# A gated attention and feed-forward block: similarity rows loaded once in the opening, TensorE's opening reordered, and the up half's banks freed by ScalarE

## The reference, cut to what matters

```python
# x, ctx: 16 x 128 x 1024, float32
def xattn(feature, embedding, weight):            # weight: 128 x 128 x 3
    emb_l = shift_right(embedding)                # zeros come in at the edge
    emb_r = shift_left(embedding)
    sim = stack([cos(embedding, emb_l), cos(embedding, embedding), cos(embedding, emb_r)], axis=1)
    att = repeat(sim, C, axis=1)                  # one row per tap, the same for all 128 channels
    inp = stack([f_pad[:, :, k:k + T] for k in range(3)], axis=2).reshape(B, 3 * C, T)
    return einsum('bit,oi->bot', inp * att, weight.reshape(O, 3 * C))

def ffn(h, gate_w, up_w, down_w, fc1_w, fc2_w, expert_w, gamma, beta):
    routing_weights, _ = top_k(h @ gate_w, 2)
    shared = relu(h @ up_w) ** 2 @ down_w         # 1024 -> 2048 -> 1024
    latent = h @ fc1_w                            # 1024 -> 512
    routed = (latent @ expert_w) * routing_weights.sum(-1, keepdims=True) @ fc2_w
    return layernorm(shared + routed) * gamma + beta

x = x + tanh(g_xattn) * xattn(layernorm(x), ctx, weight)
x = x + tanh(g_ffn) * ffn(layernorm(x), ...)
```

## Time and profile before

| | |
|---|---|
| time, median of 3 runs | 1007.84 us (1005.25 to 1008.19) |
| the profiled execution | 1008.68 us, its span 1006.5 us |
| TensorE's mean granted clock | 0.985 |
| TensorE busy | 948.0 us, 94% of the span |
| VectorE, ScalarE, GpSimd busy | 484.1, 323.2, 324.5 us |
| TensorE in the first 100 us | busy 70.44 us |
| TensorE in the next two hundreds | busy 92.10 and 91.13 us |

### The profile page before, as it was taken

How to read it: one execution, slowest core, us unless ns; L and a number is a source line. 1 busy time by engine, 2 the same in 40 slices (tenths; PEclk the granted TensorE clock), 3 DMA queues, 4 the chain that set the end, 5 groups by cost and what they waited for, 6 DMA issues and landing times.

```text
span 1006.5 us, 12367 instructions
## 1 busy us (share of the span) xinstructions
PE 948.0 (94%) x4562; PEld 441.6 (44%) x4562; DVE 484.1 (48%) x845; ACT 323.2 (32%) x441; POOL 324.5 (32%) x149
## 2 busy tenths in 40 slices
PE   2898799969999999999999999999999999999995
PEld 1346544434444444444444444444444444444442
DVE  6366588896466244455574244455574222221112
ACT  2457777553322112233332112233332112211111
POOL 4250224045954233033763333033763200001110
PEclk9899999979999999999999999999999999999998
DMA  8797797323234354423225244422225222200001
GB/s 347 206 312 262 296 384 279 113 80 105 85 96 139 106 180 152 143 90 84 58 93 144 99 160 152 141 92 84 59 90 145 77 94 102 84 1 7 15 21 42
DMA packets 63999, 131.28 MB, mean 130 GB/s; under 512 B 35266, under 2 KB 35394, under 8 KB 62658
## 3 DMA queue, kind: packets, MB, share of 16 engines
q1 hardware_dynamic: 62786, 126.07, 38.7%
q10 hardware_dynamic: 1152, 4.39, 1.2%
HBM read 105.09 MB, written 19.07 MB: 123 GB/s over the span
## 4 chain that ended last, share of the span: by engine, by line
PE 81%; DVE 9%; ACT 2%; DMA 2%; issue 2%; DVEq 2%; POOL 1%; SPq 0%; ACTq 0%; POOLq 0%
PE psS L1328 31%; PE psR L1278 18%; PE psS L1278 16%; PE psR L1338 8%; PE psP L1246 5%; PE psP L1259 2%; DVE ring L1055 1%; DVE s L893 1%; DVE hid L1106 1%; DVE s L897 1%; DMA sim_scratch<-simo 1%; PE psR L1384 1%; DMA sim_side<-sim_scratch 1%; DVEq L1092 1%; ACT hid L765 1%
## 5 line engine op out<-in xcount | busy, mean ns | idle before, releaser
L1328 PE MATMUL psS<-big,hid 128*128 128x512 f16 x1536 | 337.6, 381 | 8.9 <-issue 8.6
L1328 PEld LDWEIGHTS psS<-big,hid 128*128 128x128 f16 x1536 | 150.5, 98 | 191.4 <-issue 11.7
L1278 PE MATMUL psS<-xT,ring 128*128 128x512 f16 (+1 forms) x912 | 191.7, 370 | 3.0 <-DVE xT L1001 1.7
L1278 PE MATMUL psR<-xT,ring 128*128 128x512 f16 (+1 forms) x912 | 190.0, 368 | 0.0
L1278 PEld LDWEIGHTS psS<-xT,ring 128*128 128x128 f16 x912 | 89.8, 99 | 102.5 <-issue 4.8
L1278 PEld LDWEIGHTS psR<-xT,ring 128*128 128x128 f16 x912 | 89.2, 98 | 97.2
L517 POOL TENSOR_TENSOR y<-y,lgb 128x1024 f32<-128x1024 f32 x15 | 39.3, 2617 | 251.7 <-ACT y L655 251.7
L1019 DVE SCALAR_TENSOR_TENSOR y<-psR,rw,y 128x1024 f32<-128x1024 f32 x15 | 19.2, 1282 | 140.6 <-PE psR L1338 140.6
L1338 PE MATMUL psR<-w,lgb 128*128 128x512 f16 x384 | 85.5, 379 | 0.0
L488 POOL TENSOR_TENSOR sides<-scr 128x1024 f32<-128x1024 f32 x12 | 29.3, 2440 | 141.6 <-DMA scr<-in_ctx 141.6
L507 POOL TENSOR_TENSOR ring<-f_buf,ring 128x1024 f32<-128x1024 f32 x18 | 39.2, 2177 | 100.8 <-ACT f_buf L623 68.8
(11 more groups left out here) (196 smaller groups left out, 989.0 us busy)
## 6 DMA issues: line engine op xcount, KB each, us to landing
ring<-pair_scratch SPq DMA_DIRECT2D x60, 512.0 KB, 3.4
ring<-sim_scratch SPq DMA_DIRECT2D x18, 504.0 KB
big<-in_w_up SPq DMA_DIRECT2D x8, 1024.0 KB, 13.7
out_rows<-y SPq DMA_DIRECT2D x15, 512.0 KB, 3.0
hid<-in_w_down SPq DMA_DIRECT2D x14, 512.0 KB, 7.7
big<-in_w_down SPq DMA_DIRECT2D x14, 512.0 KB, 8.2
pair_scratch<-ring SPq DMA_DIRECT2D x12, 512.0 KB, 7.0
sim_side<-sim_scratch SPq DMA_DIRECT2D x11, 504.0 KB
```

The costliest lines, as they stand in the source:

```text
L1278: mm = pe.matmul(up_bank[t % NR][:, cols], rows[:, a, k, :], xT[:, k, b, cols], start=(k == 0 and a == 0 and b == 0), stop=(k == KB - 1 an ...
L1328: mm = pe.matmul(psS[:, HALF * h:HALF * h + HALF], hT[:, i, a, P * j:P * j + P], dn[:, i, b, HALF * h:HALF * h + HALF], start=(i == 0 and ...
```

## The change

It has six parts.

1. The first block's similarity rows are read once: one broadcast of 504 KB for row j and the three edge pieces (`load_first_sims`). VectorE copies the broadcast to the other two taps' tiles (`copy_sims`, L958 after). The taps are taken in the order `T_FIRST`, GpSimd's second one and VectorE's behind a copy each.
2. The fc1 load goes from ScalarE's queue to SP's, behind the broadcasts of rows 0 to 2, and the loads of `w_up` come in another order.
3. TensorE's opening: the attention of row 0 stands ahead of the third fc2 product, the fourth one behind the first transposes, the transposes of row 2 ahead of the first latent half tiles, and the norm of `w_up` ahead of the first latent tile's second half.
4. ScalarE's and VectorE's openings are reordered to that: all four fc1 low halves stand ahead of `combine(0, 1)`.
5. In every up half ScalarE's Relu itself frees the bank. ScalarE then squares the Relu's result out of SBUF straight into the high half, VectorE squares the same buffer in float32 (L1111 after) and takes the low half (L1119 after). The shift constants follow.
6. In the first up half `w_down` rows 0 to 9 are split beside the tiles, rows 10 to 15 (before 13 to 15) behind `f_los`, and the split stands at the end of each tile's work. The first attention of block 1 stands behind ten steps of `shared` (before twelve), and each of these steps waits for its own hidden row and its own `w_down` row (before, the whole product waited for 14 hidden rows).

```diff
-HID_SHIFT = -45
+HID_SHIFT = -23
+    T_FIRST = (0, 2, 1)
-        DN_SPLIT = {13: (0, 2), 14: (2, 4), 15: (4, 6), 16: (6, 8), 17: (8, 10), 18: (10, 12), 19: (12, 13)}
-        DN_LATE = range(13, IT)
+        DN_SPLIT = {13: (0, 2), 14: (2, 4), 15: (4, 6), 16: (6, 8), 17: (8, 10)}
+        DN_LATE = range(10, IT)
-        XATTN_AT, XATTN_FIRST = (5, 0, 0, 0), (12, 12, 10, 6)
+        XATTN_AT, XATTN_FIRST = (5, 0, 0, 0), (10, 12, 10, 6)
...
+            def load_first_sims(j):
+                rows = sim_dram[:, T * j:T * j + T]
+                S = S_first[j % 3]
+                sp.dma_start(S[0][0:G * GROUP, :],
+                             rows.rearrange("(a g) t -> a g t", a=1).broadcast_to([GROUP, G, T]))\
+                    .then_inc(sim_first[j], 16)
+                for k, ends in enumerate((slice(0, 2), slice(0, 3, 2), slice(1, 3))):
+                    sp.dma_start(S[k][G * GROUP:, :], rows[ends, :]).then_inc(sim_first[j], 16)
...
             for j in range(3):
-                load_sims(0, j)
+                load_first_sims(j)
+            sp.dma_start(fc1_flat, w_fc1.rearrange("p t k -> p (t k)")).then_inc(f1_in, 16)
...
-                    for n, k in enumerate(T_ORDER[0:2]):
+                    for n, k in enumerate(T_FIRST[0:2]):
+                        if n == 1:
+                            pool.wait_ge(s_copied, 2 * j + 1)
...
-                        act.activation(buf, bank, ACT.Relu, scale=2.0 ** HID_SHIFT).then_inc(relu_rdy, 1)
+                        act.activation(buf, bank, ACT.Relu, scale=2.0 ** HID_SHIFT).then_inc(up_evac, 1)
-                    if first:
-                        for c in range(*DN_SPLIT.get(t, (0, 0))):
-                            dn_split_hi(c)
                     if t >= LT:
-                        act.wait_ge(sq_hid, i + 1)
-                        act.activation(hT[:, t - LT, 0, :], hbuf[:, t % 2, :], ACT.Copy).then_inc(h_hi, 1)
+                        act.drain()
+                        act.activation(hT[:, t - LT, 0, :], hbuf[:, t % 2, :], ACT.Square).then_inc(h_hi, 1)
...
-            act.dma_start(fc1_flat, w_fc1.rearrange("p t k -> p (t k)")).then_inc(f1_in, 16)
...
+            def copy_sims(j):
+                dve.wait_ge(s_sem(0, j), sims_loads(0, j))
+                for k in T_FIRST[1:]:
+                    dve.tensor_copy(s_of(0, j)[k][0:G * GROUP, :], s_of(0, j)[0][0:G * GROUP, :])\
+                        .then_inc(s_copied, 1)
...
                         i = IT * n + t - LT
-                        dve.wait_ge(relu_rdy, i + 1)
-                        dve.scalar_tensor_tensor(out=hbuf[:, t % 2, :], in0=bank, scalar=0.0,
-                                                 in1=hbuf[:, t % 2, :], op0=ALU.max, op1=ALU.mult)
-                        dve.drain().then_inc(up_evac, 1)
-                        dve.drain().then_inc(sq_hid, 1)
+                        dve.wait_ge(h_hi, i + 1)
+                        dve.tensor_tensor(hbuf[:, t % 2, :], hbuf[:, t % 2, :], hbuf[:, t % 2, :], ALU.mult)
...
             def first_up_half():
                 pe.wait_ge(xt_rdy, 2 * BB)
+                norm_over_rows(WUP, IT, 3)
                 for t in range(LT):
                     tile(slot(t), t, slice(PAIR, TOK)).then_inc(up_done, 1)
-                    if t == 0:
-                        norm_over_rows(WUP, IT, 3)
...
                     if first:
+                        pe.wait_ge(h_rdy, i + 1)
                         pe.wait_ge(dn_rdy, i + 1)
...
-                        pe.wait_ge(h_rdy, IT * (n + 1) - 2)
                         if first:
                             pe.wait_ge(w2_rdy, LT)
+                        else:
+                            pe.wait_ge(h_rdy, IT * (n + 1) - 2)
```

More of the change, by code:

```diff
@@ L465, in _ @@
             for k in range(2, 4):
+                load_up(k)
+            sp.wait_ge(w2_done, LT)
+            for k in range(6, 8):
                 load_up(k)
@@ L699, in up_half @@
                             act.drain().then_inc(dn_sq, 1)
+                        for c in range(*DN_SPLIT.get(t, (0, 0))):
+                            dn_split_hi(c)
                     if first and t in CTX_FIRST:
@@ L806, in _ @@
             act.drain().then_inc(amax_rdy, 1)
-            w2_evac(2)
-            f_rows(0, 2)
-            for l in range(3):
-                w2_squares(l)
             f_rows(0, 3)
@@ L813, in _ @@
             x1_normal(0, 0)
-            w2_evac(3)
+            w2_evac(2)
+            for l in range(3):
+                w2_squares(l)
             act.wait_ge(scale_rdy, 2)
@@ L825, in _ @@
                 up_square(it)
+            w2_evac(3)
+            w2_squares(3)
             first_xt_hi(1, 0)
@@ L829, in _ @@
             x1_normal(0, 2)
-            for it in range(12, IT):
+            for it in range(4, 8):
                 up_square(it)
+            first_xt_hi(2, 0)
+            first_xt_hi(2, 1)
             std(L1, 3)
             x1_normal(0, 3)
-            first_xt_hi(2, 0)
-            first_xt_hi(2, 1)
-            for it in range(4, 6):
+            for it in range(12, IT):
                 up_square(it)
@@ L839, in _ @@
             first_xt_hi(3, 1)
-            for it in range(6, 12):
+            for it in range(8, 12):
                 up_square(it)
@@ L1098, in up_half @@
                         tile_lo(EARLY + t)
-                    if first and t == SCALE_T:
-                        down_scale()
-                    if first:
-                        for c in range(*DN_SPLIT.get(t, (0, 0))):
-                            dn_lo(c)
                     if t >= LT:
-                        dve.wait_ge(h_hi, i + 1)
+                        dve.drain()
                         dve.tensor_tensor(hT[:, t - LT, 1, :], hbuf[:, t % 2, :], hT[:, t - LT, 0, :],
@@ L1109, in up_half @@
                         x_stats(m, 0)
+                    if first and t == SCALE_T:
+                        down_scale()
                     if phase_a and t == COS_T:
                         cosines(m)
+                    if first:
+                        for c in range(*DN_SPLIT.get(t, (0, 0))):
+                            dn_lo(c)
                     if first and t == SUM_T:
@@ L1192, in _ @@
             dve.drain().then_inc(scale_rdy, 1)
+            copy_sims(3)
+            fc1_los(0, LT)
+            combine(0, 1)
             weigh_last(3)
-            combine(0, 1)
             first_xt_lo(0, 0)
             first_xt_lo(0, 1)
-            fc1_los(0, 2)
             combine(0, 2)
@@ L1392, in _ @@
             norm_over_rows(WX, 2, 1)
+            xattn_first(0)
             expert_fc2(2)
-            xattn_first(0)
-            expert_fc2(3)
             norm_over_rows(WF1, 1, 2)
@@ L1399, in _ @@
             turn_first(0, 1)
+            expert_fc2(3)
             xattn_first(2)
```

55 lines of the change are left out of this document (29 added, 26 removed).

## The result

The changed kernel takes 1015.54 us (median of 4 runs, 1014.15 to 1016.12) against 1007.79 us before: 1.0088 times as long, with a 95% interval of 1.0064 to 1.0111. The forecast was 1014.5. The profiled execution after took 1014.15 us with a span of 1012.4, 5.9 us more than the span of before.

What follows compares the result with a forecast made beforehand. TensorE was taken as the bound, busy 948.0 of 1006.5 us. Opening +7.7, end of up half -0.4, loop -0.6 give +6.7: 1015.4 profiled, 1014.5 for the median, range 1001 to 1021.

Steps and rivals of the forecast that it cites:

- the opening: Start of the kernel up to the first hidden tile: costs 7.7 us, or 2 with cheap copies and no collision.
- two signs: Wrong if the wait ahead of the first f16 attention is under 3 us, or the norm of w_up comes before 107.
- (c): TensorE's opening: row 0's attention ahead of the third fc2 product, idle 9.2 us in place of 4.70, both done at 59.3.
- (d): ScalarE behind that fc2 product: evacuation, three squares, then fc1 high halves, the first at 65.3, the last at 68.5.
- (f) to (h): From row 1's combine on: row 1 normalised at 79.3 (5.8 later), norm of w_up at 111.1, first hidden tile at 126.3.
- (a): VectorE's opening: two copies ahead of row 0's product, 1.22 us each (lower bound 0.6), end at 41.4.
- (e): VectorE's four fc1 low halves ahead of row 1's combine meet GpSimd's row 3 products: 4.6 us charged, bounds 0 to 4.6.
- The end of the up half: First up half: VectorE's stretch 108.45 us, f_los at 233.9, wait moved but no shorter, only 0.4 us given back.
- rule on the shared port: VectorE operations with two SBUF inputs and GpSimd ones reading SBUF exclude each other; 6.4 us less if not for squares.
- The loop: Later rounds: the two attention waits go as ScalarE frees banks, -0.6 us.
- the faster one: End of first up half won, VectorE 9.9 us quicker there: 1002, or 996 with the opening at its low bound; chance 0.25.

Runs made afterwards that it cites:

- comb_first: The changed kernel with VectorE's combine of row 1 put back ahead of the four fc1 low halves: 1009.48 us, 1.0026 of the kernel before.
- fill: The changed kernel with the third fc2 product put back ahead of the first attention: 1015.63 us, 1.0077 of the kernel before.
- best2: Changed kernel with row 1's combine first, both squares on ScalarE, beta's additions split, and a third opening order (third fc2 product ahead of first attention): 998.47 us.
- banks_only: The kernel before with parts 5 and 6 of the change alone, its opening untouched: 1011.82 us, 1.0049 of the kernel before.
- psum_square: The changed kernel with VectorE's square reading the PSUM bank and ScalarE's Relu, VectorE freeing the bank: 1013.42 us, 1.0064 of the kernel before.
- act_square: The changed kernel with ScalarE taking the float32 square too, VectorE keeping only the low half: 1002.37 us, 0.9948 of the kernel before.
- dn_back: The changed kernel with part 6's tables put back (three late w_down rows, attention behind 12 steps): 1016.08 us, 1.0089 of the kernel before.

## Why the forecast came out right, and where it did not

The direction and the size were right, by 1 us, and that closeness is in part luck: two errors of 4 us in opposite directions stand in the sum, the opening (+3.35 for +7.7) and row 2 (+3.8 for nothing). The prediction named two signs that would show it wrong, and one came: the norm of `w_up` starts at 106.80, before 107. The other did not: the wait ahead of the first float16 attention is 4.54, not under 3.

*The opening* was forecast at +7.7 and is +3.35 in the profiled execution, some 5 over all the profiles. Steps (c), (d) and (f) to (h) hold as differences. Attention and fc2 took 14.07 us for 14.26 (41.66 to 55.73), from there to the first fc1 high half 5.16 for 4.9, `combine` to `x1_normal` 4.94 for 4.96 (70.14 to 75.08), from there to the norm of `w_up` 31.72 for 31.85, and from the norm to the first hidden tile 15.15 for 15.15. The step that failed is (a). 1.7 us are the copies: 0.68 each, near the lower bound, where the nearest row, 1.22, was taken, and GpSimd's product needs only the first of the two. 1.6 us are VectorE, which was free earlier than in the trace of before (37.4 for 39.0); that is within the spread of the openings, so it is chance. So the attention came at 41.66, not 45.0, and all that follows is 3.3 to 4.35 us early. The 0.7 us that the prediction estimated from the Trainium skill ("VectorE: DVE Perf Modes", "The perf-mode tier table") agrees with the 0.68 of the trace.

The collision of (e) is there but smaller: the four low halves take 8.15, and 4.87 in `comb_first`, where they meet no GpSimd work, so it costs 3.3 where 4.6 were charged. From the end of the first high half to `combine` it is 8.07 us (62.07 to 70.14) where 9.0 were forecast (65.3 to 74.3). But the step's weight was put down too low: the whole block of low halves ahead of `combine(0, 1)` costs 7.2 us at row 1, as `comb_first` shows, and (c) and (d), the late fc2 product, are not what sets the first hidden tile: `fill` and `best2` put it back and gain nothing, as VectorE's copies and products beside GpSimd come to be waited for instead.

*The end of the up half.* VectorE's stretch was forecast at 108.45 and is 107.4 (121.11 to 228.51), 108.1 in `banks_only`; the split of it was off. The squares take 938 ns on the mean, not 1087, and the low halves behind them 1243 where 1087 was kept. Together 34.9 us stand where 34.8 were forecast. The Trainium skill's rule on the shared port ("SBUF — State Buffer", "SBUF: two separate sides") agrees with `psum_square`: 684 ns with one PSUM input, 938 with two SBUF inputs. That the wait moves behind ten steps and is no shorter by itself was right; it is 4.54 and not 9.9 because the opening was 4.35 earlier, the stretch 1.05 shorter, and TensorE came to it as late as forecast (shared product at 210.91, forecast 211.0).

It came that late by a step that the forecast lacks. The norm of `w_down` waits 2.38 us for VectorE, and the 24 matmuls behind it take 6.87 in place of 5.18. The prediction had put all of VectorE's lateness at `f_los` and had looked at no other place where TensorE waits for it. With `act_square` that wait is gone.

*Row 2* was not in the forecast: +3.8. ScalarE can't empty the bank of row 1 before row 0 is stored, and the last step of GpSimd's finish of row 0 comes 4.1 us later, behind the products of row 1, which wait for the six late halves of `w_down`. GpSimd before and after, then ScalarE in the changed kernel:

```profile
269.80 2.36 POOL L519 TENSOR_TENSOR y<-y,home 128x1024 f32<-128x1024 f32 x1
```

```profile
273.89 2.36 POOL L536 TENSOR_TENSOR y<-y,home 128x1024 f32<-128x1024 f32 x1
```

```profile
279.05 1.11 ACT L679 ACTIVATE y<-psS,coef 128x1024 f32<-128x1024 f32 x1 [2.02 <-DMA out_rows<-y]
```

The prediction counted those three moved halves on VectorE and not what is queued behind them: GpSimd's products, its finish and the store. How much of the 3.8 is those halves the runs don't settle: `dn_back`, with three of them late, still waits 1.21.

*The loop* was forecast at -0.6: the attentions give 0.8 (0.4 in each of two rounds), and 1.3 is lost at the start of block 2, where TensorE's wait is 2.53 for 1.22. What it waits for there no row names.

Of the rivals, the faster one needed VectorE 9.9 us quicker; `act_square` makes it 11.1 quicker and lands at 1002, the 1002 that this rival was priced at. That the two agree so well is chance too, as `act_square` has the cheaper opening and row 2's loss, which the rival had not. The squares in the loop take 908 ns on the mean and cost nothing: the waits for `f_los` there went away.

What stays open: the profiled executions differ by 5.5 us and the medians by 7.75. Some of it may be the spread of the opening; that `banks_only` runs 2.9 us above its profile is not explained.

## What to carry to other kernels

An engine that frees a bank sooner gains nothing when another engine's load sets the end of the stage: here the square moved from a PSUM to an SBUF input and kept VectorE as late as before, while giving the same square to an engine with room was worth 13 us. When a step is put ahead of another in a queue, price the whole block that now stands in front, and follow the chain behind it through the engines that are off the path, down to the store that frees a buffer. A short stall of TensorE is to be priced with the slow matmuls that may follow it.
